# A four-layer graph network on TensorE: the second aggregation goes ahead of the attention logits, and half of it changes bank

## The chip, the cores and the metric

One core of one Trainium2 chip. The metric is the device time of one execution in microseconds (us), lower is better. "Graph" below means one of the 16 batch entries.

## The reference, cut to what matters

Every graph has 512 nodes with 128 features. Four layers run one after the other, each followed by a residual and a layer norm:

```python
x = layernorm(x + L0(x, adj))    # conv of 17 taps, messages over exp(-dist) * adj, GRU gates
x = layernorm(x + L1(x, adj))    # attention: sigmoid(q k^T) * adj, normalised, times X
x = layernorm(x + L2(x, adj))    # project(expmap0(adj @ logmap0(x)))
x = layernorm(x + L3(x, adj))    # relu(D^-1/2 (adj + I) D^-1/2 (x W^T + b))
```

The change touches the product `adj @ logmap0(x)` of L2 and the logits `q k^T` of L1. logmap0 scales each row of x by artanh(norm) / norm. L2 then needs the norm of each row of the product, a tanh of it, and a row-wise scale.

## The kernel before, in words

The kernel is a software pipeline written out by hand. A slot t (`body(t, mid, rear)` on every engine) works on three graphs at once: the front of graph t (L0), the middle of graph t-1 (L1) and the rear of graph t-2 (L2 and L3). Slots 0 to 3 are unrolled, 4 to 14 run in a hardware loop, and slot 15 opens the function `ending`, which then drains the last two graphs in the steps that it calls b and c. Slots 2 to 15, fourteen of them, have both a middle and a rear. Each engine has its own program in a fixed order and meets the others through counting semaphores, `ev[...]`; a `wait_ge` holds everything behind it on the same engine. There is no planner: the order of the lines is the order of the work.

PSUM is eight named banks of 128x512 fp32, one matmul wide: CONV, F0, F1, C0, C1, K0, K1, K2. The page drops the digit of a name, so C is C0 or C1, F is F0 or F1, K is K0, K1 or K2.

TensorE's order in a slot with a rear (L1469 to L1513), as far as it matters:

- transposes of the state Y (L1352), messages, distances, taps of the convolution (L1300), transposes of the first norm, `projections` (L1379: queries into K2, keys into F0, the linear rows into K0), taps 2 to 8 of the odd half;
- `attention` (L1387): four products of 128x512, each two fp32 passes, into C0, C1, C0, C1. The third waits for the sigmoid of the first (`sig_ready`), the fourth for that of the second, because ScalarE must have emptied the bank;
- `support` (L1368): the second layer's aggregation, four chunks of four products of 128x128 each, from the adjacency ADJR and the tangent rows FX. It waits for FX (`xt_ready`), and before chunks 2 and 3 for all four sigmoids, since those chunks lie in C1 (`support_bank`, L221);
- `summed_messages` (L1398), `sum_taps`, `own_gates` (L1406: a gate into C0, then one into F0), `reset_gate_of_x`, `last_aggregation` (L1428, waits for FS by `fs_ready`), `attention_degree`, `last_linear`, `gates_of_messages` (waits for `z2_ready`), the other gates, and `attended` (the attention's aggregation), which ends the slot.

VectorE's order (L1065 to L1134), as far as it matters: statistics and norms of layers 0 and 1, the artanh factor, `leaky` (L833, makes QT and KT, the operands of the logits), `degree_guard`, `tangent` (L804, ends with FX at L818), `leaky_linear`, `masked0` (L825), `attention01` and `attention2` (L752: masks on the sigmoids 0, 1 and 2), `own_loops` (L922), `norm_guard` (L853), `ball_factor`, `second_residual` (L865, reads the four chunks of the aggregation from PSUM and makes Z2), `rest_of_messages`, `attention3`, `scaled_norm` (L925, makes FS), and the rest.

ScalarE's order (L535 to L576), as far as it matters: `queries_and_keys`, `second_norm` (L415), a logarithm, a table load, `linear` (L507), the four `sigmoids` (L459), and only then `support_norms` (L498: four squares with row sums, L501, from the aggregation's banks), `support_tanh`, `summed_messages` (L519). GpSimd does the small powers (L347 for the norm of the aggregation). SyncE issues the loads: ADJR for the next slot after `agg3_done`, ADJM after the last mask, ADJF after `a0_ready`.

Of the kernel before, what the change touches and what calls it, by code (L numbers as in the profile page):

```python
# [13 lines left out]
C = N // P  # L14
# [54 lines left out]
def adj_resnorm_kernel(nc, xT_d, adjT_d, adj_d, mask_d, weights_d, less_d, rows_d, params_d, sqmat_d, ident_d, out_d):  # L69
    ctx = ExitStack()  # L70
    with ctx:
# [3 lines left out]
        def bank(name):  # L75
            return ctx.enter_context(nc.psum_tensor(name, [P, N], F32))

        def sem(name):
            return ctx.enter_context(nc.semaphore(name))
# [79 lines left out]
        CONV, F0, F1, C0, C1, K0, K1, K2 = (bank(n) for n in ("CONV", "F0", "F1", "C0", "C1", "K0", "K1", "K2"))  # L159
# [3 lines left out]
        ev = {n: sem("s_" + n) for n in EVENTS + LN_EVENTS + DMA_EVENTS}  # L163
# [8 lines left out]
        def counts(e, t):  # L172

            n = {k: at(e, t, k) for k in (2, 1, 0, -1, -2)}
            n = {"f_next": n[2], "f": n[1], "f_prev": n[0], "m": n[0], "m_prev": n[-1], "r": n[-1],
                 "r_prev": n[-2], "first": isinstance(t, int) and t == 0, "drain": isinstance(t, int) and t >= B,
                 "last": isinstance(t, int) and t > B}
            return n

        def nth(chunk, graphs):  # L180

            n = C * graphs - (C - 1 - chunk)
            return max(0, n) if isinstance(n, int) else n

        def every(graphs):

            return C * graphs
# [27 lines left out]
        def cols(t, c):  # L215
            return t[:, c * P:(c + 1) * P]
# [2 lines left out]
            return MSG if n["drain"] else X1  # L219

        def support_bank(n, c):  # L221
            return (K0 if n["last"] else K1) if c < C // 2 else F0 if n["drain"] else C1

        def third_norm_of(n):
            return X1 if n["last"] else X3
# [17 lines left out]
        def adjacency(n):  # L243
            return ADJF if n["last"] else ADJM if n["drain"] else ADJR
# [982 lines left out]
        def _(pe):  # L1227
# [11 lines left out]
            def weight(at_col):  # L1239

                return WH[:, at_col:at_col + P], WL[:, at_col:at_col + P]
# [21 lines left out]
            def aggregate_nodes(out, adj, rows, done, chunks=range(C)):  # L1263

                for c in chunks:
                    for k in range(C):
                        last = mm(cols(out(c), c), adj[:, k, c * P:(c + 1) * P], rows[:, k, :], start=(k == 0),  # L1267
                                  stop=(k == C - 1))
                    last.then_inc(done, 1)
# [26 lines left out]
            def taps(at_col, a, b, out, high, low, count):  # L1296

                for k in range(a, b):
                    for i, (w, h) in enumerate(((WH, high), (WH, low), (WL, high))):
                        last = mm(out, w[:, at_col + k * P:at_col + (k + 1) * P], h[:, k:k + PH],  # L1300
                                  start=(k == 0 and i == 0), stop=(k == count - 1 and i == 2))
                return last
# [5 lines left out]
            def odd_taps(a, b):  # L1308

                return taps(S_ODD, a, b, CONV[:, PH:N], H1H[:, 1, :], H1L[:, 1, :], EVEN)  # L1310
# [11 lines left out]
            def gate(bank, first, last, terms):  # L1322
                k = 0
                for wgt, mov in terms:
                    for i, j in ((0, 0), (0, 1), (1, 0)):
                        k += 1
                        done = mm(bank[:, :], wgt[i], mov[j], start=(first and k == 1),  # L1327
                                  stop=(last and k == 3 * len(terms)))
                return done
# [38 lines left out]
            def support(n):  # L1368
                pe.wait_ge(ev["xt_ready"], n["r"])
                if not n["drain"]:  # L1370
                    pe.wait_ge(ev["adjr_loaded"], 16 * n["r"])
                if not n["last"]:
                    pe.wait_ge(ev["res_scaled"], n["r_prev"])
                pe.wait_ge(ev["exp_ready"], every(n["f"]))
                aggregate_nodes(lambda c: support_bank(n, c), adjacency(n), FX, ev["agg2_done"], (0, 1))
                pe.wait_ge(ev["sig_ready"], every(n["m"]))
                aggregate_nodes(lambda c: support_bank(n, c), adjacency(n), FX, ev["agg2_done"], (2, 3))

            def projections(n):  # L1379
# [7 lines left out]
            def attention(n):  # L1387
                pe.wait_ge(ev["q_ready"], n["m"])
                pe.wait_ge(ev["k_ready"], n["m"])
                for c in range(C):  # L1390
                    if c < 2:
                        pe.wait_ge(ev["exp_ready"], nth(c, n["f"]))
                    else:
                        pe.wait_ge(ev["sig_ready"], nth(c - 2, n["m"]))
                    mm(CB[c % 2][:, :], cols(KT, c), QT[:, :], start=True, stop=True).then_inc(  # L1395
                        ev["att_done"], 1)
# [9 lines left out]
            def own_gates(n):  # L1406
                if n["first"]:
                    pe.wait_ge(s_split, 5)
                pe.wait_ge(ev["sig_ready"], nth(2, n["m"]))
                gate(C0, True, False, [(weight(S_HH + P), xt)])  # L1410
                pe.wait_ge(ev["k_raw"], n["m"])
                gate(F0, True, True, [(weight(S_HH + 2 * P), xt)])

            def attention_degree(n):
# [54 lines left out]
            def body(t, mid, rear):  # L1469
                n = counts(pe, t)  # L1470
                following = not isinstance(t, int) or t + 1 < B
                if mid:
                    state_by_nodes(n)
                    messages(n)
                distances(n)
                if not mid:
                    messages(n)
                first_taps(n)
                if mid:
                    first_norm_by_features(n)  # L1480
                even_taps(8, EVEN)
                if n["first"]:
                    pe.wait_ge(s_split, 3)
                odd_taps(0, 2)
                if mid:
                    projections(n)
                odd_taps(2, 8)
                if mid:
                    attention(n)
                if rear:  # L1490
                    support(n)
                summed_messages(n)
                sum_taps(n)
                odd_taps(8, EVEN).then_inc(ev["conv2_done"], 1)
                own_gates(n)
                reset_gate_of_x(n)
                if rear:
                    last_aggregation(n)
                if mid:
                    attention_degree(n)  # L1500
                if rear:
                    last_linear(n)
                gates_of_messages(n)
                reset_gate_of_conv(n)
                if following:
                    factors(n["f_next"], n["f"])
                    first_conv(n["f_next"], n["f"])
                update_gate(n)
                if following:
                    own_squares(n["f_next"])  # L1510
                new_gate(n)
                if mid:
                    attended(n)  # L1513

            def ending():
                a, b, c = counts(pe, B - 1), counts(pe, B), counts(pe, B + 1)
                state_by_nodes(a)
                messages(a)
                distances(a)
                first_taps(a)  # L1520
                first_norm_by_features(a)
                even_taps(8, EVEN)
                odd_taps(0, 2)
                projections(a)
                odd_taps(2, 8)
                attention(a)
                support(a)
                summed_messages(a)
                sum_taps(a)
                odd_taps(8, EVEN).then_inc(ev["conv2_done"], 1)  # L1530
                own_gates(a)
                reset_gate_of_x(a)
                last_aggregation(a)
                attention_degree(a)
                gates_of_messages(a)
                reset_gate_of_conv(a)
                update_gate(a)
                new_gate(a)
                attended(a)
                state_by_nodes(b)  # L1540
                last_linear(a)

                first_norm_by_features(b)
                projections(b)
                attention(b)
                attention_degree(b)
                support(b)
                attended(b)
                last_aggregation(b)
                support(c)  # L1550
                last_linear(b)

                last_aggregation(c)
                last_linear(c)

            slots(pe, body, ending)


# [63 lines left out]
```

## Time and profile before

| what | value |
|---|---|
| median of 3 runs | 773.96 us (771.95 to 775.07) |
| the profiled execution | 773.77 us, span 772.0 us |
| TensorE matmul busy | 709.7 us, 92% |
| VectorE busy | 625.5 us, 81% |
| ScalarE busy | 423.6 us, 55% |
| GpSimd busy | 138.0 us, 18% |
| mean granted TensorE clock | 0.976 of full |
| from one slot to the next | 43.7 us (FX is made at 102.19, the last time in a slot at 670.94, 13 slots on) |

The span is what the trace covers, from the first instruction to the last; the execution's own time is 1.8 us longer. A busy matmul is one that was in flight, since starts overlap: an fp32 product of 128x512 shows two matmuls, which start 0.43 us apart. Where a row of the timeline says x8, it merges eight neighbours, and its second column runs from the first start to the last end.

### The profile page before, as it was taken

What the parts mean: (1) busy time and instruction counts of PE and PEld (TensorE: products, weight loads), DVE (VectorE), ACT (ScalarE), POOL (GpSimd) and SP (SyncE); (2) the same over time, 40 slices, a digit from 0 to 9 for tenths busy, and PEclk for the clock granted to TensorE, in tenths of its full rate; (3) what the DMA queues carried; (4) which work ended last, traced back from release to release, by engine and by line L of the source; (5) the groups of instructions that cost most, each with busy time, mean ns of one, the idle gap of its engine ahead of it and who ended that gap; (6) DMA issues with size and microseconds to landing.
All of it is one profiled execution on the core that took longest, in us unless ns stands there. A gap on an engine that the chain in (4) does not pass through costs nothing.

```text
span 772.0 us, 12824 instructions
## 1 busy us (share of the span) xinstructions
PE 709.7 (92%) x3984; PEld 547.4 (71%) x3984; DVE 625.5 (81%) x2080; ACT 423.6 (55%) x881; POOL 138.0 (18%) x151
## 2 busy tenths in 40 slices
PE   3879999999999999999999999999999999998553
PEld 1757877777787867777787867778687777775531
DVE  7456788888888888888888888888888888876655
ACT  4153754747374665748375665738465565734431
POOL 0000121221121111122121111112121121111221
PEclk9999999999999999999999999999999999998886
DMA  5304333150614233160513234060523324101000
GB/s 204 123 0 134 113 110 110 65 182 14 207 39 149 82 122 122 34 211 14 183 62 128 103 110 135 16 228 14 177 68 119 112 81 164 56 15 55 5 10 28
DMA packets 46585, 75.33 MB, mean 98 GB/s; under 512 B 4064, under 2 KB 12768, under 8 KB 46432
## 3 DMA queue, kind: packets, MB, share of 16 engines
q1 hardware_dynamic: 46560, 75.02, 28.9%
q8 instruction: 12, 0.20, 0.1%
q14 instruction: 13, 0.11, 0.0%
HBM read 70.82 MB, written 4.19 MB: 97 GB/s over the span
## 4 chain that ended last, share of the span: by engine, by line
PE 81%; ACT 10%; DVE 5%; issue 3%; POOL 1%; DMA 0%; SPq 0%; ACTq 0%; POOLq 0%; DVEq 0%
PE K L1267 11%; PE C L1395 7%; PE F L1403 7%; PE C L1327 7%; PE K L1432 7%; PE CONV L1300 6%; PE K L1300 6%; PE F L1327 6%; ACT JUNKD L487 5%; PE K L1260 4%; PE C L1267 3%; ACT A L454 3%; PE K L1381 2%; PE K L1287 2%; PE F L1383 2%
## 5 line engine op out<-in xcount | busy, mean ns | idle before, releaser
L337 POOL TENSOR_TENSOR RSTD<-VEPS,POW 128x4 f32<-128x4 f32 x48 | 48.9, 1019 | 276.7 <-DVE VEPS L687 276.7
L1300 PE MATMUL CONV<-H1H,WH 128*128 128x256 f32 x288 | 84.5, 293 | 0.0
L1300 PE MATMUL CONV<-H1L,WH 128*128 128x256 f32 x288 | 81.7, 284 | 0.0
L1300 PE MATMUL CONV<-H1H,WL 128*128 128x256 f32 x288 | 81.4, 283 | 0.0
L1395 PE MATMUL C<-QT,KT 128*128 128x512 f32 x128 | 62.0, 609 | 0.0
L1267 PEld LDWEIGHTS K<-XS,BIG 128*128 128x128 f32 x496 | 57.8, 192 | 1.3
L1267 PE MATMUL K<-XS,BIG 128*128 128x128 f32 x496 | 57.9, 275 | 0.0
L1403 PE MATMUL F<-A,MSG 128*128 128x512 f32 x128 | 57.6, 592 | 0.0
L1300 PEld LDWEIGHTS CONV<-H1L,WH 128*128 128x128 f32 x288 | 55.4, 192 | 0.6
L1300 PEld LDWEIGHTS CONV<-H1H,WH 128*128 128x128 f32 x288 | 55.3, 192 | 0.7
L1300 PEld LDWEIGHTS CONV<-H1H,WL 128*128 128x128 f32 x288 | 55.3, 192 | 0.0
L1432 PE MATMUL K<-ADJR,FS 128*128 128x512 f32 x112 | 50.4, 592 | 0.0
L459 ACT ACTIVATE BIG<-C 128x512 f32<-128x512 f32 x64 | 38.0, 596 | 15.6 <-PE C L1395 14.2
L1300 PE MATMUL K<-HSH,WH 128*128 128x256 f32 x128 | 42.5, 332 | 0.0
L1395 PEld LDWEIGHTS C<-QT,KT 128*128 128x128 f32 x128 | 21.9, 190 | 28.6 <-ACT BIG L459 19.5
L454 ACT ACTIVATE A<-C 128x512 f32<-128x512 f32 x32 | 17.4, 596 | 42.5 <-PE C L1339 42.5
L825 DVE TENSOR_TENSOR A<-A,ADJF 128x512 f32<-128x512 f32 x64 | 39.9, 685 | 0.0
L1403 PEld LDWEIGHTS F<-A,MSG 128*128 128x128 f32 x128 | 23.2, 190 | 23.4 <-issue 23.4
L752 DVE TENSOR_TENSOR BIG<-BIG,ADJM 128x512 f32<-128x512 f32 x60 | 39.8, 683 | 0.0
L487 ACT ACTIVATE JUNKD<-ADJN 128x512 bf16<-128x512 f32 x64 | 39.6, 641 | 0.0
L409 ACT ACTIVATE XH<-X_IN 128x512 fp32r<-128x512 f32 x16 | 10.1, 631 | 53.4 <-PE F L1327 53.4
L352 POOL TENSOR_TENSOR D<-D,POW 128x4 f32<-128x4 f32 x16 | 16.1, 1008 | 123.7 <-DVE D L947 123.7
(262 smaller groups left out, 1966.1 us busy)
## 6 DMA issues: line engine op xcount, KB each, us to landing
ADJF<-in_adjT SPq DMA_DIRECT2D x16, 1024.0 KB, 5.3
ADJN<-in_adj SPq DMA_DIRECT2D x16, 1024.0 KB, 7.6
ADJM<-in_adjT SPq DMA_DIRECT2D x15, 1024.0 KB, 5.6
ADJR<-in_adjT SPq DMA_DIRECT2D x14, 1024.0 KB, 5.2
X_IN<-in_xT SPq DMA_DIRECT2D x16, 256.0 KB, 2.6
out<-OUT SPq DMA_DIRECT2D x16, 256.0 KB, 2.7
BIG<-in_weights SPq DMA_DIRECT2D x1, 1088.0 KB, 5.2
BIG<-in_weights SPq DMA_DIRECT2D x1, 576.0 KB, 9.0
```

The source lines that it names most:

```text
L337: nc.gpsimd.tensor_tensor(RSTD[:, row, :], VEPS[:, row, :], POW[:, 0, :], ALU.pow).then_inc(ev[f"ln{layer}_rstd"], 1)
L454: A(A0[:, c, :], DB[c][:, :], ACT.Exp).then_inc(ev["exp_ready"], 1)
L459: A(SIG[:, c, :], CB[c % 2][:, :], ACT.Sigmoid, scale=float(P) ** -0.5).then_inc(ev["sig_ready"], 1)
L487: last = A(JUNKD[:, c, :], ADJN[:, c, :], ACT.Copy, accum_out=DEG[:, c:c + 1])
L752: last = V.tensor_tensor(A1[:, c, :], SIG[:, c, :], attention_adjacency(n)[:, c, :], ALU.mult)
L825: last = V.tensor_tensor(A0[:, c, :], A0[:, c, :], ADJF[:, c, :], ALU.mult)
L1267: last = mm(cols(out(c), c), adj[:, k, c * P:(c + 1) * P], rows[:, k, :], start=(k == 0), stop=(k == C - 1))
L1300: last = mm(out, w[:, at_col + k * P:at_col + (k + 1) * P], h[:, k:k + PH], start=(k == 0 and i == 0), stop=(k == count - 1 and i == 2))
L1327: done = mm(bank[:, :], wgt[i], mov[j], start=(first and k == 1), stop=(last and k == 3 * len(terms)))
L1395: mm(CB[c % 2][:, :], cols(KT, c), QT[:, :], start=True, stop=True).then_inc(ev["att_done"], 1)
L1403: last = mm(F1[:, :], MSG[:, c, :], A0[:, c, :], start=(c == 0), stop=(c == C - 1))
L1432: last = mm(last_sums_bank(n)[:, :], FS[:, k, :], adjacency(n)[:, k, :], start=(k == 0), stop=(k == C - 1))
```

## The change

Three edits. In `support_bank` chunks 2 and 3 go to F0 in every slot (in the drain they did already), where the keys lay until ScalarE copied them out; the wait before them is now for that copy (`k_raw`) in place of the four sigmoids. `own_gates` gets a wait for `z2_ready` before its gate into F0. And `support` is called ahead of `attention` in the slots and in slot 15.

```diff
         def support_bank(n, c):
-            return (K0 if n["last"] else K1) if c < C // 2 else F0 if n["drain"] else C1
+            return (K0 if n["last"] else K1) if c < C // 2 else F0
...
                 aggregate_nodes(lambda c: support_bank(n, c), adjacency(n), FX, ev["agg2_done"], (0, 1))
-                pe.wait_ge(ev["sig_ready"], every(n["m"]))
+                pe.wait_ge(ev["k_raw"], n["m"])
                 aggregate_nodes(lambda c: support_bank(n, c), adjacency(n), FX, ev["agg2_done"], (2, 3))
...
                 pe.wait_ge(ev["k_raw"], n["m"])
+                pe.wait_ge(ev["z2_ready"], every(n["r"]))
                 gate(F0, True, True, [(weight(S_HH + 2 * P), xt)])
...
                 odd_taps(2, 8)
+                if rear:
+                    support(n)
                 if mid:
                     attention(n)
-                if rear:
-                    support(n)
                 summed_messages(n)
...
                 odd_taps(2, 8)
+                support(a)
                 attention(a)
-                support(a)
                 summed_messages(a)
```

## Rows read from the trace of the kernel before

**Rows 1.** The page: busy time by engine, and the chain that ended last by engine

```profile
PE 709.7 (92%) x3984; PEld 547.4 (71%) x3984; DVE 625.5 (81%) x2080; ACT 423.6 (55%) x881; POOL 138.0 (18%) x151
...
PE 81%; ACT 10%; DVE 5%; issue 3%; POOL 1%; DMA 0%; SPq 0%; ACTq 0%; POOLq 0%; DVEq 0%
```

**Rows 2.** Stages of slot 8: stretch, its us, busy PE, PEld, DVE, ACT, POOL, clock, DMA

```profile
371.60:380.30 8.70, 8.70 (x46) 6.42 (x45) 7.22 (x29) 2.96 (x10) 2.02 (x2) 1.00 0.72 247
380.30:395.90 15.60, 15.56 (x85) 11.83 (x83) 13.35 (x35) 9.45 (x13) 2.75 (x3) 1.00 0.36 133
```

**Rows 3.** Timeline of slot 8, TensorE matmuls: start, us, line, operands, count

```profile
364.36 3.86 PE L1395 MATMUL C<-QT,KT 128*128 128x512 f32 x8
368.05 1.95 PE L1267 MATMUL K<-FX,ADJR 128*128 128x128 f32 x16
...
371.62 3.60 PE L1403 MATMUL F<-A,MSG 128*128 128x512 f32 x8
...
380.38 3.17 PE L1432 MATMUL K<-ADJR,FS 128*128 128x512 f32 x7
```

**Rows 4.** Timeline of slot 8, weight loads; in brackets the idle time before, and its releaser

```profile
352.15 0.42 PEld L1352 LDWEIGHTS F<-IDENT,Y 128*128 128x128 f32 x4 [0.23 <-DVE Y L766]
...
364.25 0.30 PEld L1395 LDWEIGHTS C<-QT,KT 128*128 128x128 f32 x2
...
366.23 0.30 PEld L1395 LDWEIGHTS C<-QT,KT 128*128 128x128 f32 x2 [0.82 <-ACT BIG L459]
...
380.15 0.42 PEld L1432 LDWEIGHTS K<-ADJR,FS 128*128 128x128 f32 x2
```

**Rows 5.** Timeline of slot 8, VectorE

```profile
351.40 0.69 DVE L766 TENSOR_TENSOR Y<-NG,XT 128x512 f32<-128x512 f32 x1
...
364.67 0.69 DVE L818 TENSOR_TENSOR FX<-X,T 128x512 f32<-128x512 f32 x1
...
368.74 1.29 DVE L752 TENSOR_TENSOR BIG<-BIG,ADJM 128x512 f32<-128x512 f32 x2
...
375.83 0.34 DVE L869 SCALAR_TENSOR_TENSOR Z<-C,T,X 128x128 f32<-128x128 f32 x1
...
378.85 1.11 DVE L935 TENSOR_SCALAR FS<-Z,NMEAN,D 128x127 f32<-128x127 f32 x4
...
384.80 0.16 DVE L945 COPY D<-K 128x4 f32<-128x4 f32 x1 [0.43 <-PE K L1420]
```

**Rows 6.** FX in all slots (tile view: least, median, most ns), and timeline of slot 15

```profile
L818 DVE TENSOR_TENSOR FX<-X,T x16: 691/691/693, 102.2 to 739.7; 128x512 f32<-128x512 f32 x16
...
670.94 0.69 DVE L818 TENSOR_TENSOR FX<-X,T 128x512 f32<-128x512 f32 x1
...
670.60 3.85 PE L1395 MATMUL C<-QT,KT 128*128 128x512 f32 x8
```

**Rows 7.** Timeline of slot 8, ScalarE: linear rows, sigmoids, squares of the aggregation

```profile
365.09 0.60 ACT L507 ACTIVATE XRAW<-K 128x512 f32<-128x512 f32 x1
365.58 1.29 ACT L459 ACTIVATE BIG<-C 128x512 f32<-128x512 f32 x2
367.39 0.60 ACT L459 ACTIVATE BIG<-C 128x512 f32<-128x512 f32 x1 [0.52 <-PE C L1395]
...
371.82 0.28 ACT L501 ACTIVATE JUNK<-C 128x128 bf16<-128x128 f32 x1 [1.16 <-PE C L1267]
...
372.09 0.27 ACT L501 ACTIVATE JUNK<-C 128x128 bf16<-128x128 f32 x1
```

**Rows 8.** Stages around the projections, in slot 8 and in the drain; columns as in rows 2

```profile
359.50:362.40 2.90, 2.87 (x14) 1.92 (x15) 2.58 (x16) 2.08 (x4) 1.37 (x2) 1.00 0.00 0
...
704.70:710.10 5.40, 5.35 (x13) 3.27 (x13) 3.04 (x15) 1.19 (x2) 1.84 (x2) 0.50 0.00 0
```

**Rows 9.** Timeline of TensorE: idle time before matmuls, in slot 8 and in the drain

```profile
359.53 1.13 PE L1381 MATMUL K<-X1T,WF 128*128 128x512 f32 x2 [0.53 <-ACT X1T L481]
...
702.77 1.28 PE L1254 MATMUL CONV<-IDENT,MSG 128*128 128x128 f32 x4 [2.51 <-DVE MSG L693]
```

## The prediction

> **What bounds the kernel now.** I read the page first, for who is busy and who is on the chain that ended last. TensorE is in flight for 92% of the span and carries 81% of the chain, ScalarE 10%, VectorE 5% [rows 1]. An average doesn't say whether a stage has slack, so next came the stages of one slot in the middle, slot 8. From 371.60 to 395.90, which is from the end of the aggregation to the end of the slot, TensorE is busy for 8.70 + 15.56 = 24.26 of 24.30 us [rows 2]. So in that stretch whatever makes TensorE later makes the slot longer, and nothing behind it can give the time back. Last came the timelines of each engine around the two blocks that change places, since the question is a race: has each operand arrived when TensorE gets there? The slots repeat closely: FX lasts 691 ns in all 16 graphs, and in slot 15 it starts 0.34 us after the first logits, in slot 8 0.31 us after them [rows 3, 5, 6].
>
> **Part one, what the move takes away.** Logits three and four wait for the sigmoids one and two to empty their banks. The loads sat idle for 0.82 us there [rows 4], but loads run ahead of matmuls, so that isn't the loss. The matmuls tell: the block starts at 364.36 and the next at 368.05, 3.69 us for eight. Undisturbed fp32 passes go 0.43 us apart (3.60 less one matmul of 0.59, over the seven steps of the summed messages [rows 3]), which makes 3.44. The stall is 0.25 us a slot. It comes from ScalarE, which did the linear rows at 365.09 and began the sigmoids 0.49 us later [rows 7]. With the logits moved back by some 4.7 us ScalarE will be idle when they come. But a bank still has to be emptied between its two uses. The third logits start at 368.05 - 1.72 = 366.33 and end at 367.19, and their sigmoid starts at 367.39, so the handover is 0.20; a sigmoid lasts 0.60 [rows 7]. The third logits are then free to load 0.86 + 0.20 + 0.60 + 0.05 = 1.71 after the first ones began, and start 0.1 us after the load (364.25 against 364.36 [rows 3, 4]), at 1.81 in place of 1.72. So 0.10 of the 0.25 stays, and the gain is 0.15 us. The wait for all sigmoids before chunks 2 and 3, which the edit replaces by `k_raw`, costs nothing today: the second half ends 3.57 us after 368.05, at 371.62, exactly when sixteen pairs do at full pace (32 products of 0.11). Its removal brings nothing.
>
> **Part two, the wait that appears.** The aggregation needs FX. VectorE finishes it at 364.67 + 0.69 = 365.36 [rows 5]. TensorE is at the place at 364.25, where it now loads the weights of the first logits [rows 4]. Handover from VectorE to a load is 0.06 (Y ends at 352.09, its load is at 352.15 [rows 4, 5]), and 0.11 from load to matmul, so the aggregation starts at 365.53 and not at 364.36: **+1.17 us**. Before, the logits hid this: their own operands QT and KT come earlier in VectorE's order than FX. Everything else on TensorE is queued behind this wait, the logits first of all. Can the time to FX shrink relative to TensorE? Both run from Y: TensorE passes through the transposes, the distances and the projections, VectorE through its statistics, factors and FX, and neither path is edited. In slot 15 the same sum is 671.63 + 0.17 - 670.60 = 1.20 [rows 6].
>
> The aggregation (3.57) then ends at 369.10, the logits (3.54) at 372.64, and the summed messages begin there in place of 371.62: 1.02 later.
>
> **Part three, the norms of the aggregation.** The aggregation itself is ready earlier, at 369.1, but ScalarE does the four squares behind the four sigmoids, and these now wait for logits that end at 372.64. The fourth sigmoid starts at 372.84, the first square 0.49 later (the step between ScalarE's neighbours, 365.09 to 365.58), the last one 3 x 0.27 on (371.82 to 372.09), at 374.14. It started at 372.09 [rows 7]. From it hang, one after the other, GpSimd's power, the tanh, the ball factor, the residual, its statistics, another power and FS. VectorE waits inside that chain, and it is now also idle between the end of `masked0` (about 368.8) and the first new sigmoid (some 370.7, mask at 368.74 before [rows 5]), so the chain shifts as a whole by 2.05 us: Z2 of the last chunk from 376.17 to 378.2, FS from 379.96 to 382.01 [rows 5].
>
> Who waits? The new wait for `z2_ready` in `own_gates`: the gate into F0 is due on TensorE some 8 us after the summed messages' start, near 380, and Z2 is there at 378.2, so it costs nothing; its cover is 1.8 us, and beyond that it would cost one for one. The **last aggregation** waits for FS: TensorE loads for it at 380.15 and starts at 380.38 [rows 3, 4], which after the delay would be 381.40. FS allows a load at 382.07 and a matmul at 382.18: **+0.78 us**. Today the margin is only 0.14 (380.15 against 380.01).
>
> After that VectorE is 2.05 late and TensorE 1.80. VectorE has 0.43 us of idle before L945 [rows 5], so it fits within the delay of TensorE. The gates of messages wait for all sigmoids and `z2_ready`, both long there. Queues: TensorE issues no DMA. SyncE's load of ADJR waits for `agg3_done` as before, now some 1.8 us later, and the next use comes a slot later; ADJM waits for the last mask, some 2 us later, for a use 30 us on. GpSimd's queue keeps its order and only gets its power later. I put all of it at nothing; the DMA share is 0 on the chain [rows 1].
>
> **Sum.** A slot gets 1.17 - 0.15 + 0.78 = 1.80 us longer. Fourteen slots have the aggregation and the logits, 2 to 15; the drain's order isn't edited. 14 x 1.80 = 25.2 us, on the profiled execution's 773.77: **799.0 us**, 3.3% more. That execution stands 0.2 us under the median, 773.96, which is nothing. Bounds for the unknown pieces: the FX wait from 1.0 (no lead of the load lost) to 1.3; what stays of the sigmoid stall from 0 to 0.25; the FS wait from 0.5 to 1.0. That is 1.25 to 2.30 us a slot, 791 to 806.
>
> **Rivals.**
>
> *FX alone.* The norm chain is absorbed: if the four squares ran between sigmoids as their waits allow, or the margin at FS were larger than the 0.14 seen. Against it: ScalarE's program puts them after all four. Each slot then pays 1.17 - 0.15 = 1.02, in all 14.3 us: 788.
>
> *VectorE paces the slot.* It loses some 1.9 us of useful time at the first mask, and has little idle time in the rest. If the 0.43 at L945 isn't enough, the reset gate and Y follow VectorE's delay of 2.05 plus another few tenths: 2.4 us a slot, 34 us, 807. Against it: the two waits on TensorE at the slot's end leave room.
>
> *The clock falls.* In slots it stays at 1.00, that is 2.4 GHz, although TensorE was idle for 0.53 us before the projections; in the drain, after 2.51 us of idle time and more around it, it is 0.50, that is 1.2 GHz, and the same projections take 5.40 us in place of 2.90 [rows 8, 9]. If the new waits of 1.17 and 0.78 us brought that on, each slot would lose another 2.5 us, 35 us in all: 834. Against it: both are shorter than the gap in the drain, and full work lies between them.
>
> The Trainium skill ("TensorE: Matmul & The Clock Gate", the part on the two states) says that the clock is one of two levels and goes by how busy TensorE has recently been; the trace agrees, with 1.00 in the slots and 0.50 in the drain [rows 8]. By that rule two more idle spells bring a slot nearer to the low level, and if they reach it the time is that of this rival.
>
> *Not slower.* The wait for FX doesn't appear, and only the gain of part one is left. Its place is the start of the aggregation, its price the 1.17 us, and it decides at the point where TensorE comes there at 365.36 or later: its path from Y would have to be 1.1 us longer than now while the slot is not. The norm chain would have to keep its time too, which it can where the squares' later start is made up by VectorE's idle time behind it. At its best this is 14 x 0.15 = 2.1 us less: 771.7. Against it: nothing ahead of that place is edited, and the four squares stay behind the four sigmoids.
>
> **How the numbers follow.** The main case 0.76, FX alone 0.10, VectorE's pace 0.06, the clock 0.02, not slower 0.06. About 0.5% (3.9 us) is what a measurement of this kernel can tell from no change. The last case falls mostly within it, so faster 0.02, same 0.04, slower 0.94. The likeliest time is 799. The range takes in the bounds of the main case and FX alone at its lower end: 788 to 807.
>
> **What the changed profile would show.** In a slot: the aggregation's first load with idle time of over 1 us put down to FX L818, then the logits with no more than 0.1 us lost; VectorE idle for near 2 us before L752, put down to a sigmoid; the squares in one row of four right behind the sigmoids; TensorE's load for the last aggregation released by FS; a slot of 45.5 us in place of 43.7; no wait of the gate into F0. I am wrong if TensorE reaches the aggregation after FX, if the FS wait is missing (then 788), or if the idle time at the slot's end has moved from TensorE's own work to VectorE's.

## The result, and the profile after

The changed kernel takes 801.56 us (801.37 to 803.24, 4 runs) against 774.52 us for the kernel before on the same chip (771.95 to 775.33, 4 runs): ratio 1.0359, 95% interval 1.0337 to 1.0381. It is 3.6% slower; 799 was forecast. The profiled execution has a span of 801.4 us, 29.4 more than before.

The page of the changed kernel, the lines that answer to [rows 1]:

```profile
PE 714.5 (89%) x3984; PEld 546.5 (68%) x3984; DVE 627.0 (78%) x2080; ACT 422.2 (53%) x881; POOL 138.0 (17%) x151
...
PE 53%; DVE 29%; issue 8%; ACT 6%; POOL 2%; DMA 0%; DVEq 0%; SPq 0%; POOLq 0%; ACTq 0%
```

By this page no engine has more instructions (TensorE's time in flight reads 4.8 us more, VectorE's busy time 1.5 us more), but TensorE's part of the chain fell from 81% to 53% and VectorE's rose from 5% to 29%: the chain now leaves TensorE twice in a slot. The timeline of TensorE shows where. Slot 8 again, as in [rows 3] (start, us, line, operands, count, idle time and releaser in brackets; the lines below L1411 are one number higher than before):

```profile
372.48 1.12 PE L1381 MATMUL K<-X1T,WF 128*128 128x512 f32 x2 [0.53 <-ACT X1T L481]
373.44 1.02 PE L1383 MATMUL F<-X1T,WF 128*128 128x512 f32 x2
...
378.64 2.05 PE L1267 MATMUL K<-FX,ADJR 128*128 128x128 f32 x16 [1.17 <-DVE FX L818]
380.52 1.95 PE L1267 MATMUL F<-FX,ADJR 128*128 128x128 f32 x16
382.31 3.70 PE L1395 MATMUL C<-QT,KT 128*128 128x512 f32 x8
385.85 3.60 PE L1403 MATMUL F<-A,MSG 128*128 128x512 f32 x8
...
393.21 0.39 PE L1327 MATMUL F<-XH,WH 128*128 128x512 f32 x1
...
395.33 3.67 PE L1433 MATMUL K<-ADJR,FS 128*128 128x512 f32 x8 [0.55 <-DVE FS L935]
...
407.14 3.73 PE L1267 MATMUL K<-XS,BIG 128*128 128x128 f32 x32
```

Two rows of the kernel before that the next readings need, the keys' product and `attended` of its slot 8:

```profile
360.49 1.02 PE L1383 MATMUL F<-X1T,WF 128*128 128x512 f32 x2
...
392.12 3.73 PE L1267 MATMUL K<-XS,BIG 128*128 128x128 f32 x32
```

The row of X1T is unchanged against [rows 9]. Two idle times are new: the aggregation waits for FX, the last aggregation for FS. The Trainium skill ("Perfetto Trace Analysis", section "Per-engine timelines") says that the profiler models TensorE's end times and doesn't observe them, so I measure this engine from start to start. From the keys' product (L1383) to the first block behind it: 378.64 - 373.44 = 5.20, before 3.87 (from 360.49 to 364.36). Both blocks together: 7.21, before 7.26. From the summed messages to the last aggregation: 9.48, before 8.76. From there to `attended`: 11.81, before 11.74. The slot is 1.33 - 0.05 + 0.72 + 0.07 = 2.07 us longer, 45.81 in place of 43.74.

VectorE and ScalarE of the same slot, answering to [rows 5, 7]:

```profile
377.62 0.69 DVE L818 TENSOR_TENSOR FX<-X,T 128x512 f32<-128x512 f32 x1
...
384.00 0.69 DVE L752 TENSOR_TENSOR BIG<-BIG,ADJM 128x512 f32<-128x512 f32 x1 [2.23 <-ACT BIG L459]
...
391.06 0.34 DVE L869 SCALAR_TENSOR_TENSOR Z<-F,T,X 128x128 f32<-128x128 f32 x1
...
394.07 1.11 DVE L935 TENSOR_SCALAR FS<-Z,NMEAN,D 128x127 f32<-128x127 f32 x4
...
399.82 0.16 DVE L945 COPY D<-K 128x4 f32<-128x4 f32 x1 [0.22 <-PE K L1421]
```

```profile
386.05 0.60 ACT L459 ACTIVATE BIG<-C 128x512 f32<-128x512 f32 x1 [0.26 <-PE C L1395]
386.54 0.27 ACT L501 ACTIVATE JUNK<-K 128x128 bf16<-128x128 f32 x1
...
387.29 0.30 ACT L501 ACTIVATE JUNK<-F 128x128 bf16<-128x128 f32 x1
```

The squares run right behind the fourth sigmoid, though both halves of the aggregation had been there since about 382.3. VectorE idles for 2.23 us ahead of the first mask. FX to FS was 14.18 us and is 16.45: the norm chain is 2.27 us longer (2.05 was forecast; the aggregation started 0.16 us later after FX than forecast and took 0.10 us longer, which is about the rest). VectorE still has 0.22 us of idle time at L945. The stages behind the FS wait, as in [rows 2]:

```profile
385.85:395.33 9.48, 8.93 (x46) 6.28 (x44) 7.96 (x31) 4.43 (x16) 2.02 (x2) 1.00 0.51 174
395.33:410.90 15.57, 15.54 (x82) 11.85 (x82) 13.56 (x35) 8.99 (x13) 2.74 (x3) 1.00 0.37 133
```

TensorE is busy again for 15.54 of 15.57 us, so VectorE doesn't pace the slot's end. The granted clock stays at 1.00 in spite of both waits, in these stages and in the one with the FX wait:

```profile
364.36:385.85 21.49, 19.75 (x131) 15.86 (x130) 17.17 (x64) 12.65 (x27) 3.86 (x4) 1.00 0.14 46
```

### The profile page after: what moved, and what is told of

It is laid out like the page before. It is cut to its first block, busy times and chain, and to the rows that moved or that the text cites. A ratio compares the mean times of both kernels' runs of the same rounds, so it can differ in the third digit from the quotient of the medians.

```text
span 801.4 us, 12851 instructions
## 1 busy us (share of the span) xinstructions
PE 714.5 (89%) x3984; PEld 546.5 (68%) x3984; DVE 627.0 (78%) x2080; ACT 422.2 (53%) x881; POOL 138.0 (17%) x151
## 4 chain that ended last, share of the span: by engine, by line
PE 53%; DVE 29%; issue 8%; ACT 6%; POOL 2%; DMA 0%; DVEq 0%; SPq 0%; POOLq 0%; ACTq 0%
PE K L1267 11%; PE K L1433 7%; PE C L1395 7%; PE C L1327 6%; PE F L1267 3%; PE F L1327 3%; DVE Z L869 2%; ACT JUNK L501 2%; DVE FS L935 2%; POOL T L347 2%; PE K L1287 2%; PE CONV L1300 2%; PE K L1442 2%; DVE Z L1002 2%; PE K L1421 2%
## 5 line engine op out<-in xcount | busy, mean ns | idle before, releaser
L1395 PE MATMUL C<-QT,KT 128*128 128x512 f32 x128 | 59.8, 608 | 0.0
L1433 PEld LDWEIGHTS K<-ADJR,FS 128*128 128x128 f32 x112 | 20.1, 189 | 33.9 <-issue 33.9
L1267 PE MATMUL K<-FX,ADJR 128*128 128x128 f32 x224 | 28.7, 281 | 15.6 <-DVE FX L818 15.6
L347 POOL TENSOR_TENSOR T<-T,POW 128x4 f32<-128x4 f32 x16 | 16.1, 1007 | 151.6 <-ACT JUNK L501 151.6
```

Source lines behind the costliest of these rows:

```text
L347: nc.gpsimd.tensor_tensor(T[:, 17, :], T[:, 16, :], POW[:, 1, :], ALU.pow).then_inc(ev["nu_pow"], 1)
L1433: last = mm(last_sums_bank(n)[:, :], FS[:, k, :], adjacency(n)[:, k, :], start=(k == 0), stop=(k == C - 1))
```

## The experiments

My theory: the cost is two waits, one for FX (the place of the aggregation) and one for FS (the squares behind the sigmoids). Rivals: the shared bank, a VectorE that paces the slot, a price of the order itself.

**The bank alone** (`bank_only`), order as before:

```diff
-            return ... F0 if n["drain"] else C1
+            return ... F0
-                pe.wait_ge(ev["sig_ready"], every(n["m"]))
+                pe.wait_ge(ev["k_raw"], n["m"])
...
                 pe.wait_ge(ev["k_raw"], n["m"])
+                pe.wait_ge(ev["z2_ready"], every(n["r"]))
                 gate(F0, True, True, [(weight(S_HH + 2 * P), xt)])
```

> The kernel before with the aggregation's second half in F0, its wait for the keys' copy in place of the four sigmoids, and the gate into F0 behind the second residual, but the order of before (logits first). My theory (the cost is the wait for FX and, behind it, the wait for FS; the bank is free): no change, 774.5 us within 0.3%. Rival (sharing F0 costs, because the gate into F0 waits for the second residual or the aggregation for the copy of the keys): a part of the 27 us, over 780 us, with an idle row ahead of the gate into F0.

Measured 773.97 us, ratio 1.0000 (0.9976 to 1.0024). The bank and its two waits are free in the old order. The order alone, with C1, can't be tried: the second logits would wait in C1 for VectorE's residual, which waits for the squares, which stand behind the sigmoids of those logits.

**The squares first** (`norms_first`), on the changed kernel:

```diff
+                if rear:
+                    support_norms(n)
                 if mid:
                     sigmoids(n, 0, C)
                 if rear:
-                    support_norms(n)
                     support_tanh(n)
```

> The changed kernel with one move on ScalarE: the four squares of the aggregation ahead of the four sigmoids. My theory: the squares then hang on the aggregation, the chain to FS starts when VectorE is through its masks, FS comes about 1 us earlier and TensorE's wait for it (0.55 us idle, 0.7 us in start times) is gone: 14 x 0.75 = 10.5 us less, 791 us. The wait for FX stays at 1.2 us. Rival (VectorE, idle for 2.2 us before the first mask, paces the slot): no more than 2 us gained, 800 us.

Measured 791.83 us, ratio 1.0234 (1.0188 to 1.0280): 9.7 us less than the changed kernel. TensorE's timeline of this kernel, from the FX wait to the last aggregation, which has no idle time now:

```profile
373.15 2.05 PE L1269 MATMUL K<-FX,ADJR 128*128 128x128 f32 x16 [1.17 <-DVE FX L820]
...
380.36 3.60 PE L1405 MATMUL F<-A,MSG 128*128 128x512 f32 x8
389.12 3.60 PE L1435 MATMUL K<-ADJR,FS 128*128 128x512 f32 x8
```

From 380.36 to 389.12 is 8.76, exactly as before the change, and the slot is 45.02. VectorE still idles for 2.23 us ahead of the masks, so that idle time costs nothing by itself. The FX wait is untouched.

**FX first** (`fx_early`), on the changed kernel:

```diff
 ScalarE
-                    queries_and_keys(n)
                     second_norm(n)
                     artanh_log(n)
+                    queries_and_keys(n)
 VectorE
-                    leaky(n)
-                    degree_guard(n)
                     tangent(n)
+                    leaky(n)
+                    degree_guard(n)
```

> The changed kernel with FX brought forward: on ScalarE the second norm and the logarithm ahead of the copies of queries and keys, on VectorE the tangent factor and FX ahead of QT and KT. My theory: FX is ready within 0.1 us of TensorE's arrival, the 1.3 us at the aggregation go, the chain to FS shifts with them, and FS is still about 0.9 us late against before, of which 0.6 to 0.7 us is seen on TensorE: 14 x 1.3 = 18 us less, 783 us. Rival (the wait for FX is only a symptom of a VectorE that paces the slot): the time moves into the other wait and the kernel stays above 795 us.

Measured 788.95 us, ratio 1.0200 (1.0155 to 1.0246): 12.6 us less than the changed kernel, against 18 expected. Two sizes were off. FX is not quite early enough, and the FS wait didn't shrink at all:

```profile
367.38 0.69 DVE L818 TENSOR_TENSOR FX<-X,T 128x512 f32<-128x512 f32 x1
...
368.41 2.05 PE L1268 MATMUL K<-FX,ADJR 128*128 128x128 f32 x16 [0.19 <-issue]
...
375.61 3.60 PE L1404 MATMUL F<-A,MSG 128*128 128x512 f32 x8
385.09 3.67 PE L1434 MATMUL K<-ADJR,FS 128*128 128x512 f32 x8 [0.56 <-DVE FS L935]
```

The profile puts the 0.19 us of idle time down to "issue", but FX ends at 368.07 and the first matmul comes 0.34 us later, as in the changed kernel (0.33), so FX still sets the time. From the keys' product (364.19) to the aggregation is 4.22, 0.35 more than before the change; from the summed messages to the last aggregation is 9.48, as in the changed kernel. That second stretch is rigid: the squares follow the fourth logits and so do the summed messages, so when FX comes earlier both ends move together. I had let the FS wait shrink with it.

**Both moves** (`both`):

> Both moves at once in the changed kernel: squares ahead of the sigmoids, FX ahead of QT and KT. My theory: both waits are gone and what is left is the small gain at the logits (0.15 us a slot) against 0.1 us of lost lead on the loads: 773 to 776 us, the kernel before within 0.3%. Rival (a third cost of the order itself, such as VectorE's idle time before the first mask): over 780 us.

Measured 777.18 us, ratio 1.0039 (1.0016 to 1.0063), 1.2 us above the range that was expected and below the rival's 780. The two repairs give back 24.4 of the 27.0 us. The slot is 44.02, 0.28 longer than before; in it VectorE waits 0.32 us for the logarithm, for which ScalarE waits behind its second norm.

**The logarithm inside the second norm** (`both_log`), on top of both moves:

```diff
+                for c in range(C):
+                    if c == C - 1:
+                        artanh_log(n)
+                    A(X2[:, c, :], Z1[:, c, :], ...)
```

> The kernel with both moves, and the logarithm on ScalarE put ahead of the fourth chunk of the second norm, so that VectorE doesn't wait 0.32 us for it before the tangent factor. In the run with both moves the aggregation still began 0.36 us later than the logits of before, and the slot was 0.28 us longer. My theory: that rest is the same wait for FX, and goes to 0.05 us: 14 x 0.3 = 4.2 us less than the 777.2 of both moves, 773 us, the kernel before within 0.3%. Rival (the rest is a price of the order, not of FX): 777 us again.

Measured 772.80 us, ratio 0.9984 (0.9965 to 1.0003); slot 43.75. With the waits for FX and FS mended the kernel is level with the one before: the loss was these two waits.

**Waits in another order** (`fx_wait_last`), on the changed kernel:

```diff
             def support(n):
-                pe.wait_ge(ev["xt_ready"], n["r"])
...
                 pe.wait_ge(ev["exp_ready"], every(n["f"]))
+                pe.wait_ge(ev["xt_ready"], n["r"])
```

> The changed kernel with the wait for FX as the last of the aggregation's four waits and not the first. In the changed kernel the first matmul comes 0.32 us after FX ends in the eleven slots of the hardware loop, but 0.05 to 0.07 us after it in the unrolled slots 2, 3 and 15, where the other waits' counts are constants. Theory: in the loop the register steps that work out those counts stand behind the wait for FX and run only when it is over; put ahead of it they hide in the wait, and the handover in the loop falls to 0.07 us: 11 x 0.25 = 2.7 us less, 798 to 799 us. Rival (the 0.25 us are something else of the loop): 801.6 us again, and 0.32 us in the trace.

FX and the first matmul in slot 3 (unrolled) of the changed kernel; slot 8 (loop) is above:

```profile
148.71 0.69 DVE L818 TENSOR_TENSOR FX<-X,T 128x512 f32<-128x512 f32 x1
...
149.45 2.05 PE L1267 MATMUL K<-FX,ADJR 128*128 128x128 f32 x16 [0.93 <-DVE FX L818]
```

Slot 8 of this kernel:

```profile
376.96 0.69 DVE L818 TENSOR_TENSOR FX<-X,T 128x512 f32<-128x512 f32 x1
...
377.80 2.02 PE L1267 MATMUL K<-FX,ADJR 128*128 128x128 f32 x16 [0.98 <-DVE FX L818]
```

The handover is 149.45 - 149.40 = 0.05 us in the unrolled slot, 378.64 - 378.31 = 0.33 in the loop, and 377.80 - 377.65 = 0.15 in the loop with FX waited for last. The view of single source lines also lists instructions that don't count as busy: ALU_OP is a register step, EVENT_SEMAPHORE a wait that is an instruction of its own (PEldq: TensorE's sequencer; duration in ns, first and last start in us). For the lines of the three waits behind the one for FX (`adjr_loaded` L1371, `res_scaled` L1373, `exp_ready` L1374) in the changed kernel, between the end of FX and the first matmul of slot 8:

```profile
L1371 PEldq ALU_OP  x1: 32/32/32, 378.3 to 378.3; - x1
L1373 PEldq EVENT_SEMAPHORE  x1: 51/51/51, 378.4 to 378.4; - x1
L1374 PEldq ALU_OP  x1: 32/32/32, 378.6 to 378.6; - x1
```

In slot 3 the same lines have no register step, and their two waits ran before FX was there, at 146.3 and 146.4. In this kernel, slot 8, what is left between FX and the matmul is the wait for FX itself (now L1374), which has become an instruction of its own:

```profile
L1374 PEldq EVENT_SEMAPHORE  x1: 51/51/51, 377.7 to 377.7; - x1
```

It is there in all 16 graphs, and the handover is 0.14 to 0.15 us in unrolled slots too. So the theory holds for the loop, but the 0.07 us that it promised were not reached, and the unrolled slots lost 0.1 us each at this place (slot 3 went from 45.71 to 45.77). In the loop the slot fell from 45.81 to 45.60. The runs give 801.31 us, ratio 1.0345 (1.0323 to 1.0367), whose interval overlaps the changed kernel's: 0.3 us less, where 798 to 799 us was expected and eleven slots should give 2.3 us. In the profiled execution the slots' gain is there (the last Y starts at 725.2 in place of 727.3) and the drain behind it took it back, 76.2 us in place of 74.1. So the wait order is shown per slot, and its worth for the whole kernel is not shown.

**A kernel without the 0.53 us at the projections.** [Rows 9] show TensorE idle for X1T, which ScalarE copies only after four row sums of the adjacency. `degrees_late`, on the kernel before:

```diff
 ScalarE
-                    degrees(n)
                 if mid:
                     first_norm_by_features(n)
...
                     sigmoids(n, 0, C)
                 if rear:
-                    support_norms(n)
+                    degrees(n, 0, 2)
+                    support_norms(n, 0, 2)
+                    degrees(n, 2, 3)
+                    support_norms(n, 2, C)
+                    degrees(n, 3, C)
 VectorE: degree_guard behind ball_factor; GpSimd: degree_power behind norm_power
```

> The kernel before (its own order and banks), with the four row sums of the adjacency on ScalarE taken from ahead of the copy of the transposed first norm into the idle time around the squares of the aggregation, and the degree's guard and power behind the norm's. TensorE idles 0.53 us a slot for that copy. Theory: what bounds the slot there is ScalarE's queue; TensorE gets 0.45 to 0.53 us a slot back, 14 x 0.5 = 7 us: 767 to 768.5 us. Rival (QT and KT on VectorE, ready 0.5 us ahead of the logits, or the squares' chain take it back): 774 us.

Measured 767.82 us, ratio 0.9921 (0.9903 to 0.9939). The idle time for X1T is gone, and 0.30 us of idle time is back as a wait for KT:

```profile
357.25 1.02 PE L1391 MATMUL F<-X1T,WF 128*128 128x512 f32 x2
...
361.57 3.79 PE L1403 MATMUL C<-QT,KT 128*128 128x512 f32 x8 [0.30 <-DVE KT L847]
```

Measured from start to start, the stretch from Y's transposes to the keys' product fell from 8.34 to 7.55 us, which is 0.79 and more than the 0.53 of idle time; 0.45 of it came back in the reach to the logits (4.32 in place of 3.87), and both blocks together take 0.06 less. The slot is 0.40 shorter. The expected time was met, but by a larger gain and a larger loss than the theory had: its rival, QT and KT, was in part true.

The row sums moved late in the new order too (`all_moves`; two of them around the squares, two behind the sigmoids), and then with the waits reordered (`all_moves_last`):

> The order of the change with all moves: squares ahead of the sigmoids, FX ahead of QT and KT, logarithm inside the second norm, row sums late. If FX bounds the new order, TensorE reaches the aggregation 0.5 us earlier, but FX, which hangs on VectorE's and GpSimd's chain from Y, does not come earlier: the wait for FX grows to 0.5 us and the time stays at 772 to 774 us, 5 us slower than the row sums' move in the old order. Rival (the new order is at par once its waits are mended): 768 us, the same as that one.

> The same reordering of waits in the kernel of the new order with all moves, where TensorE waits some 0.7 us for FX and the handover in the loop is 0.33 us too. Theory: 11 x 0.25 = 2.7 us less than its 773.1 us, 770 to 771 us, and still slower than the same row sums' move in the old order (767.8 us), since the wait for FX itself stays at 0.4 us or more. Rival: 773 us again.

Measured 773.14 us, ratio 0.9988 (0.9972 to 1.0005), and 771.66 us, ratio 0.9962 (0.9945 to 0.9980). The first of them, where the aggregation waits:

```profile
361.59 0.69 DVE L837 TENSOR_TENSOR FX<-X,T 128x512 f32<-128x512 f32 x1
...
362.61 2.05 PE L1286 MATMUL K<-FX,ADJR 128*128 128x128 f32 x16 [0.71 <-DVE FX L837]
```

What TensorE gains at X1T it waits again for FX: from Y's transposes to the keys' product is 7.54, 0.79 less than in `both_log`, and from there to the aggregation is 4.74, 0.80 more. In `all_moves_last` the handover is again 0.15 and the loop's slot 43.53 in place of 43.75; the intervals of the two kernels just overlap, so here too its worth for the whole kernel is not shown. In the old order the logits stand there, and their operands are earlier. So `series_late` goes on with the old order: in `degrees_late`, QT and KT ahead of the artanh series, which only FX needs.

```diff
                     artanh_ratio(n)
-                    artanh_series(n)
                 if mid:
                     leaky(n)
                 if rear:
+                    artanh_series(n)
                     tangent(n)
```

> The kernel with the late row sums in the old order, and on VectorE QT and KT ahead of the six small steps of the artanh series, which only FX needs. There the logits now wait 0.30 us for KT while FX has over 2 us in hand. If each operand has to be ready in the order in which TensorE asks for it, the series costs nothing behind KT: the 0.30 us go, 14 x 0.3 = 4 us less, 763 to 765 us. Rival (the logits' start is also held by the sigmoids' bank or the squares' chain): 767 to 768 us again.

Measured 762.78 us, ratio 0.9846 (0.9820 to 0.9872): faster than both kernels, and 0.2 us below the range that was expected. FX and TensorE's timeline:

```profile
355.52 1.02 PE L1391 MATMUL F<-X1T,WF 128*128 128x512 f32 x2
...
359.38 3.85 PE L1403 MATMUL C<-QT,KT 128*128 128x512 f32 x8
...
360.41 0.69 DVE L826 TENSOR_TENSOR FX<-X,T 128x512 f32<-128x512 f32 x1
...
363.07 1.95 PE L1275 MATMUL K<-FX,ADJR 128*128 128x128 f32 x16
```

No wait is left there: 3.86 us from the keys' product to the logits, as before, and the slot is 42.95. FX ends at 361.10 and is asked for at 363.07.

The slots of all kernels side by side (us; the reach is from the keys' product to the next block behind the taps):

```
kernel           reach   both blocks   to last agg.   slot    median us
before           3.87    7.26          8.76           43.74   774.52
bank_only        3.87    7.26          8.76           43.74   773.97
changed          5.20    7.21          9.48           45.81   801.56
fx_wait_last     5.02    7.18          9.47           45.60   801.31
norms_first      5.20    7.21          8.76           45.02   791.83
fx_early         4.22    7.20          9.48           44.83   788.95
both             4.23    7.20          8.75           44.02   777.18
both_log         3.94    7.20          8.76           43.75   772.80
all_moves        4.74    7.21          8.75           43.75   773.14
all_moves_last   4.54    7.18          8.76           43.53   771.66
degrees_late     4.32    7.20          8.76           43.34   767.82
series_late      3.86    7.26          8.77           42.95   762.78
```

## Why the prediction was right

**The bound.** TensorE's order behind the two blocks has no slack: the two delays came through to the slot's end, and only they did.

**Part one, the gain at the logits.** From 382.31 to 385.85 is 3.54, where 3.54 was forecast and 3.69 stood before: 0.15, as worked out. That the wait for the sigmoids was worth nothing is shown by `bank_only`.

**Part two, the wait for FX.** Forecast 1.17, measured 1.33 plus 0.10 in the aggregation's own length (382.31 - 378.64 = 3.67, before 3.57), because after the wait the first load and the first matmul start together (378.63 and 378.64), where I had the load ahead. My 0.17 for handover and load is 0.05 + 0.10 in the unrolled slots 2 and 3, so that estimate held there; these slots grew by 1.86 and 1.91 us. In the loop the handover is 0.33. This is the one term that was mis-sized: some 0.25 us in eleven slots, 2.8 us. I took the handover from Y. Its wait is followed by one more, but both take the graph's number as it is, and no register step stands between Y and its load. The wait for FX is the first of four, and in the loop two register steps and a wait stand behind it. `fx_wait_last` moved 0.18 us of it.

**Part three, the norms.** Forecast 0.78 at the last aggregation. Measured 0.72, and 0.07 more behind it in the block's own length. `norms_first` takes it away whole. The gate into F0 found Z2 ready 1.8 us ahead (391.40; that gate starts at 393.21). VectorE's idle time ahead of the masks was 2.23 where I had about 1.9.

**Sum.** Forecast 1.80 a slot and 25.2 us; measured 2.07 in the loop, that is 1.80 plus 0.25 for the register steps and rounding. From the first Y to the last the profiled executions differ by 29.7 us, of which 1.0 lies in slot 1, which the change doesn't touch (over the profiled executions of all twelve kernels it took from 35.7 to 38.2 us). The medians of the runs differ by 27.0, less than the 28.8 of the fourteen slots; the profiled execution of the changed kernel was the slowest of its four. The forecast 799 stands 2.6 under the median, and a part of its closeness is luck: by the slots of the trace it is 3.6 short.

**The rivals.** FX alone fell with the FS wait in the trace, and `norms_first` priced it at 9.7 us. VectorE's pace fell with the 0.22 us of idle time left at L945 and with 45.02 in `norms_first`, where its idle time stayed and the slot shrank. It was close: 0.43 had become 0.22. The clock fell with 1.00 in the three stages above. The Trainium skill ("TensorE: Matmul & The Clock Gate", section "What's actually happening") lets the clock go by how busy TensorE has been; waits of 1.17 and 0.55 us among some 44 us of work don't change it here, and a drain with longer gaps runs at 0.77. Not slower fell with the first run.

## What to carry to other kernels

Before a block moves up an in-order engine, compare for each of its operands the time when it is ready with the time when the engine would ask, and follow what stands behind the block in the consumers' queues: here the squares waited in ScalarE's program for sigmoids that had moved behind them. The move cost nothing here only once the producers' orders had moved with it, and even then the new order wasn't better than the old one given the same move of the row sums (771.66 us against 767.82); what helped was to bring the producers' order in line with the old one. In a loop whose counts are computed, try the wait that ends last as the last one before the instruction: here it took 0.18 us off the handover in the loop and added 0.1 in unrolled code.

## What the runs showed of the hardware

- In the hardware loop a wait cost more than in unrolled code when others with computed counts followed it: 0.33 us from the end of FX to the first matmul against 0.05 us, with two register steps of 32 ns and a semaphore instruction of 51 ns in between. With that wait put last the handover was 0.15 us in the loop and in unrolled slots alike.
- The drain, the same code in all these kernels up to small moves, varies by more than 2 us. From the start of the last Y to the end of the span it was 74.1 to 74.7 us in seven kernels (74.3 before, 74.1 changed, 74.7 `degrees_late`) at a mean granted clock of 0.77 to 0.78, 75.3 in `all_moves_last` at 0.76, and 76.2 to 76.8 in four (`fx_early`, `fx_wait_last`, `all_moves`, `series_late`) at 0.74. I didn't find what decides it; the kernels with the longer drain aren't those with one certain edit. It is as large as what some of the edits were worth, so I compared slots and not spans.
